# Two-layer graph network on 12,500 nodes: six tiles a round gathered ahead instead of three, and source counts compared against a row in PSUM

## The reference, cut to what matters

```python
def _L0_gnn_ref(feat, W1, W2, b, src, dst):
    out_deg = jnp.maximum(jax.ops.segment_sum(ones, src, num_segments=n), 1.0)
    in_cnt = jax.ops.segment_sum(ones, dst, num_segments=n)
    t1 = feat @ W1
    msg = t1[src] + feat[src] * feat[dst] @ W2
    scale = jnp.sqrt(out_deg[src]) * jnp.sqrt(out_deg[dst])
    agg = jax.ops.segment_sum(msg / scale[:, None], dst, num_segments=n)
    embed = jnp.where(in_cnt[:, None] > 0, t1 + agg, jnp.zeros_like(t1)) + b
    embed = jax.nn.leaky_relu(embed, negative_slope=0.01)
    return embed / jnp.maximum(jnp.linalg.norm(embed, axis=1, keepdims=True), 1e-12)

def _L1_gnn_ref(x, W, b, edge_index):
    src, tgt = (edge_index[0], edge_index[1])
    xt = jnp.einsum('ni,oi->no', x, W) + b
    out = jax.ops.segment_sum(xt[src], tgt, num_segments=num_nodes)
    deg = jax.ops.segment_sum(jnp.ones_like(tgt, dtype=x.dtype), tgt, num_segments=num_nodes)
    return out / (deg + 1.0)[:, None]

x = _layernorm(x + _L0_gnn_ref(x, L0_gnn_W1, L0_gnn_W2, L0_gnn_b, src, dst), axis=-1)
x = _layernorm(x + _L1_gnn_ref(x, L1_gnn_W, L1_gnn_b, edge_index), axis=-1)
```

## Time and profile before

| | us |
|---|---|
| median of three runs | 4066.2 |
| lowest and highest run | 4062.96, 4067.36 |
| span of the profiled execution, first to last instruction | 4061.9 |
| GpSimd busy | 3038.5 (75%) |
| TensorE busy, matmuls | 3098.3 (76%) |
| VectorE busy | 1691.2 (42%) |
| mean granted TensorE clock, share of full speed | 0.758 |

### The profile page before, as it was taken

How to read it: one execution, slowest core, us unless ns; L and a number is a source line. 1 busy time by engine, 2 the same in 40 slices (tenths; PEclk the granted TensorE clock), 3 DMA queues, 4 the chain that set the end, 5 groups by cost and what they waited for, 6 DMA issues and landing times.

```text
span 4061.9 us, 41375 instructions
## 1 busy us (share of the span) xinstructions
PE 3098.3 (76%) x9904; PEld 1794.2 (44%) x9904; DVE 1691.2 (42%) x3546; ACT 518.9 (13%) x1597; POOL 3038.5 (75%) x3147
## 2 busy tenths in 40 slices
PE   6527777777777777777768887887888787888887
PEld 5414554455455554545434443333444343344433
DVE  9934444444444554444432333333332333333323
ACT  8911111111111111111100000000000000000000
POOL 7867777777777777777757777777777777777776
PEclk8758888888888888888866677767676767666666
DMA  7584444444444444444424434344444444444443
GB/s 253 157 280 133 138 131 132 138 138 135 134 133 138 138 133 135 133 138 137 124 86 115 120 115 120 115 120 115 120 117 118 117 118 117 117 119 116 120 115 106
DMA packets 281951, 536.08 MB, mean 132 GB/s; under 512 B 60499, under 2 KB 181892, under 8 KB 281924
## 3 DMA queue, kind: packets, MB, share of 16 engines
q0 software_dynamic: 150048, 409.93, 35.3%
q1 hardware_dynamic: 119204, 112.98, 8.7%
q10 hardware_dynamic: 12672, 12.85, 0.9%
HBM read 478.55 MB, written 56.97 MB: 132 GB/s over the span
## 4 chain that ended last, share of the span: by engine, by line
POOL 69%; issue 24%; PE 2%; SPq 1%; DMA 1%; DVE 1%; POOLq 1%; DVEq 1%; ACT 0%; ACTq 0%
POOL ring L474 65%; POOL ring L482 4%; SPq L321 1%; PE banks L1116 1%; PE banks L1090 1%; DVEq L678 1%; DMA ring<-scaled_x,idx 0%; POOLq L503 0%; POOLq L471 0%; DMA ring<-in_x,src_col 0%; POOLq L472 0%; DMA ring<-in_dst 0%; DVE stats L903 0%; SPq L287 0%; DVE out_t L899 0%
## 5 line engine op out<-in xcount | busy, mean ns | idle before, releaser
L1116 PE MATMUL banks<-ring,hot_space 128*128 128x257 f32 x6252 | 2628.9, 542 | 852.9 <-DMA ring<-scaled_x,idx 389.4
L1116 PEld LDWEIGHTS banks<-ring,hot_space 128*128 128x128 f32 x6252 | 1328.2, 249 | 2077.5 <-DMA ring<-x,idx 1053.7
L474 POOL DMA_INDIRECT ring<-x,idx x1563 | 1487.2, 951 | 504.6 <-issue 475.9
L474 POOL DMA_INDIRECT ring<-scaled_x,idx x1422 | 1350.7, 950 | 442.5 <-issue 440.1
L836 DVE SCALAR_TENSOR_TENSOR big<-banks,here_mask,big 128x257 f32 x784 | 343.7, 480 | 1833.5 <-PE banks L1116 1833.4
L796 DVE TENSOR_TENSOR hot_space<-banks,dst_rel 128x1024 f32<-128x1024 f32 x395 | 483.6, 1225 | 210.1 <-issue 207.1
L582 ACT COPY idx<-src_col 128x8 int32 (+1 forms) x392 | 77.3, 197 | 2350.1 <-PE banks L1116 2350.1
L482 POOL DMA_INDIRECT ring<-in_x,src_col x141 | 196.0, 1390 | 57.4 <-issue 42.4
L1090 PE MATMUL banks<-w_s,a_t 128*128 128x256 f32 x784 | 187.0, 394 | 0.0
L1090 PEld LDWEIGHTS banks<-w_s,a_t 128*128 128x128 f32 x784 | 156.6, 200 | 23.8 <-ACT a_t L604 0.4
L546 ACT ACTIVATE dst_rel<-columns,halves 128x128 bf16<-128x128 f32 x576 | 161.3, 375 | 3.2 <-DVE halves L715 3.2
(11 more groups left out here) (115 smaller groups left out, 958.7 us busy)
## 6 DMA issues: line engine op xcount, KB each, us to landing
ring<-x,idx POOLq DMA_INDIRECT x1563, 2.8
ring<-scaled_x,idx POOLq DMA_INDIRECT x1422, 2.8
kept_rows<-ring SPq DMA_DIRECT2D x141, 128.0 KB, 3.3
ring<-kept_rows SPq DMA_DIRECT2D x47, 384.0 KB, 3.8
x<-out_t SPq DMA_DIRECT2D x98, 128.0 KB, 2.4
x_t<-x SPq DMA_DIRECT2D x98, 128.0 KB, 2.2
x_t<-in_x SPq DMA_DIRECT2D x97, 128.0 KB, 2.2
result<-out_t SPq DMA_DIRECT2D x97, 128.0 KB, 1.9
```

The costliest lines, as they stand in the source:

```text
L474: g.indirect_dma_start(ring[:, u, 0:D], None, table[layer], bass.IndirectOffsetOnAxis(ap=idx[:, u:u + 1], axis=0)).then_inc(rows_in[u], 16)
L1116: last = nc.tensor.matmul(group_sum(k % SUMS), dst_hot[:, k % HOTS, u - k * GT, :], ring[:, u, 0:DW], start=u == tiles[0], stop=u == tiles ...
```

## The change

1. `KEPT` goes from 3 to 6. 282 tiles are gathered early, and rounds 1 to 47 of layer 0 gather 26 tiles where they gathered 29. The load of kept rows, their scaling, and the look-up of `r_kept` become twice as wide.
2. Kept tiles are gathered into blocks of three that lie side by side in the flat `ring` (11 blocks, `UNITS`), and a block goes out with one store of 384 KB, 94 stores in all.
3. The comparisons of the source counts take a row of numbers that stands in PSUM (`lane_row`) in place of the table `count_to` in SBUF, and lay their results out one tile behind the other. There are 70 such batches where there were 80, and 112 batches of signs where there were 72. TensorE's loop over them is written out.
4. The edges are staged in the last columns of x's own buffer, so that `ring` is free from the start; the first six kept tiles read their source numbers from `first_src`, loaded by a DMA of its own ahead of the edges.
5. x is loaded, scaled and stored in 14 chunks of 7 blocks where there were 8 of up to 14.
6. The memset of the ones in `ring` waits for the last kept store.

```diff
@@ -46,12 +46,10 @@
 HB = 16
-PAIR = 2
 SB = 4
-STEP_BATCHES = 72
+STEP_BATCHES = 112
...
-SPANS = 8
@@ -64,15 +62,18 @@
 FINAL = -(-EDGES // P) - (ROUNDS - 1) * U
-X_CHUNKS = [(w, min(w + 14, NW)) for w in range(-8, NW, 14)]
-X_CHUNKS[0] = (0, X_CHUNKS[0][1])
...
-KEPT = 3
+X_CHUNKS = [(w, w + 7) for w in range(0, NW, 7)]
...
+KEPT = 6
...
-SLOTS = 16
-BASES_AT = 82
+UNIT = 3
+KEPT_UNITS = KEPT_TILES // UNIT
+UNITS = U * PITCH // (UNIT * D)
+X_EVERY = 4
+BASES_AT = 78
+NAT_AT = NW * D - 4 * BLOCKS * P
@@ -98,8 +99,11 @@
         ring_flat = ring[:, :, :].rearrange("p u f -> p (u f)")
-        nat = [ring_flat[:, n * BLOCKS * P:(n + 1) * BLOCKS * P] for n in range(2)]
-        nat_i = [ring_flat[:, (2 + n) * BLOCKS * P:(3 + n) * BLOCKS * P].bitcast(I32) for n in range(2)]
+        early = [ring_flat[:, n * UNIT * D:(n + 1) * UNIT * D] for n in range(UNITS)]
+        staging = big[:, NAT_AT:NW * D]
+        nat = [staging[:, n * BLOCKS * P:(n + 1) * BLOCKS * P] for n in range(2)]
+        nat_i = [staging[:, (2 + n) * BLOCKS * P:(3 + n) * BLOCKS * P].bitcast(I32) for n in range(2)]
+        first_src = sb("first_src", [P, KEPT], I32)
@@ -107,16 +111,14 @@
         place_hot = dst_col[:, 0:KE]
-        place_low = dst_col[:, KE:2 * KE].bitcast(I32)
-        place_src = dst_col[:, 2 * KE:3 * KE].bitcast(I32)
-        count_to = sb("count_to", [P, P, PAIR], BF16)
+        place_src = dst_col[:, KE:2 * KE].bitcast(I32)
...
-            "p (h a n c) -> p h a n c", h=2, a=HB // PAIR, c=PAIR)
+            "p (h t n) -> p h t n", h=2, t=HB)
...
-        lo_hot = [hot[:, n, :, 0:P, :] for n in range(2)]
-        hi_hot = [hot[:, n, :, P:P + HI, :] for n in range(2)]
+        lo_hot = [hot[:, n, :, 0:P] for n in range(2)]
+        hi_hot = [hot[:, n, :, P:P + HI] for n in range(2)]
@@ -156,8 +158,9 @@
         out_t = [sb(f"out_t{n}", [P, D]) for n in range(2)]
-        sums_t = sb("sums_t", [P, 2, DW])
-        block_hot = sums_t[:, :, :].rearrange("p s f -> p (s f)")[:, 0:KEPT * NW].rearrange("p (t n) -> p t n", t=KEPT)
+        sums_space = sb("sums_space", [P, KEPT * NW])
+        sums_t = sums_space[:, 0:2 * DW].rearrange("p (s f) -> p s f", s=2)
+        block_hot = sums_space[:, :].rearrange("p (b t n) -> p b t n", b=2, t=UNIT)
@@ -176,7 +179,7 @@
         project = [banks[:, 6, s * D:(s + 1) * D] for s in range(2)]
-        found = banks[:, 2, 0:KEPT * NW].rearrange("p (t n) -> p t n", t=KEPT)
+        found = banks[:, 2:4, 0:UNIT * NW].rearrange("p b (t n) -> p b t n", t=UNIT)
@@ -278,6 +282,8 @@
                 sp.sem_inc(stored[s], 16)
+            sp.dma_start(first_src[:, :], src[U * P:U * P + KE].rearrange("(t p) -> p t", p=P),
+                         allow_slow_non_contiguous=True).then_inc(first_in, 16)
@@ -288,10 +294,10 @@
                              edges[FULL_TILES * P:EDGES].rearrange("(p e) -> p e", p=1)).then_inc(edges_loaded[n], 16)
-            sp.wait_ge(x_padded, 1)
...
+                if end * D > NAT_AT:
+                    sp.wait_ge(x_padded, 1)
@@ -316,16 +322,16 @@
             def store_kept(n):
-                slot = n % SLOTS
-                sp.wait_ge(early_in[slot], 16 * (n // SLOTS + 1))
-                sp.dma_start(kept[n // KEPT, :, n % KEPT * D:(n % KEPT + 1) * D],
-                             ring[:, slot, 0:D]).then_inc(kept_out[slot], 16)
-
-            for n in range(KEPT_TILES):
+                place, half = n % UNITS, n % (KEPT // UNIT)
+                sp.wait_ge(early_in[place], 16 * UNIT * (n // UNITS + 1))
+                sp.dma_start(kept[n * UNIT // KEPT, :, half * UNIT * D:(half + 1) * UNIT * D],
+                             early[place]).then_inc(kept_out[place], 16)
+
+            for n in range(KEPT_UNITS):
                 store_kept(n)
-                if n % 4 == 1 and n // 4 < len(X_CHUNKS):
-                    load_x_chunk(*X_CHUNKS[n // 4])
-                if n == 4 * len(X_CHUNKS):
+                if n % X_EVERY == 0 and n // X_EVERY < len(X_CHUNKS):
+                    load_x_chunk(*X_CHUNKS[n // X_EVERY])
+                if n == X_EVERY * len(X_CHUNKS):
@@ -476,19 +480,23 @@
             def gather_kept(n):
-                slot, tile = n % SLOTS, (n // KEPT + 1) * U + n % KEPT
-                if n >= SLOTS:
-                    g.wait_ge(kept_out[slot], 16 * (n // SLOTS))
-                g.indirect_dma_start(ring[:, slot, 0:D], None, x,
-                                     bass.IndirectOffsetOnAxis(ap=src_col[:, tile:tile + 1], axis=0)
-                                     ).then_inc(early_in[slot], 16)
-
+                place, t = n // UNIT % UNITS, n % UNIT
+                if t == 0 and n >= UNITS * UNIT:
+                    g.wait_ge(kept_out[place], 16 * (n // (UNITS * UNIT)))
+                tile = (n // KEPT + 1) * U + n % KEPT
+                sources = first_src[:, n:n + 1] if n < KEPT else src_col[:, tile:tile + 1]
+                g.indirect_dma_start(early[place][:, t * D:(t + 1) * D], None, x,
+                                     bass.IndirectOffsetOnAxis(ap=sources, axis=0)).then_inc(early_in[place], 16)
+
+            g.wait_ge(first_in, 16)
+            for n in range(KEPT):
+                gather_kept(n)
+            g.wait_ge(edges_in_cols, 1)
+            for n in range(KEPT, KEPT_TILES):
+                gather_kept(n)
+            for place in range(UNITS):
+                g.wait_ge(kept_out[place], 16 * len(range(place, KEPT_UNITS, UNITS)))
             g.wait_ge(idx_ready, 4)
-            g.wait_ge(step_digits_made, 1)
-            for n in range(KEPT_TILES):
-                gather_kept(n)
-            for slot in range(SLOTS):
-                g.wait_ge(kept_out[slot], 16 * len(range(slot, KEPT_TILES, SLOTS)))
@@ -551,6 +559,8 @@
                     step_batch(3 * b + third, third)
+            for n in range(STEP_BATCHES // 3 * 3, STEP_BATCHES):
+                step_batch(n, n % 3)
@@ -681,10 +691,9 @@
                 for digit, hots, size in ((src_lo, lo_hot, P), (src_hi, hi_hot, HI)):
-                    vals = digit[:, bass.ds(batch * HB, HB)].rearrange("p (a c) -> p a c", c=PAIR)
-                    shape = [P, HB // PAIR, size, PAIR]
-                    last = nc.vector.tensor_tensor(hots[half], vals.unsqueeze(2).to_broadcast(shape),
-                                                   count_to[:, 0:size, :].unsqueeze(1).to_broadcast(shape), ALU.is_equal)
+                    vals = digit[:, bass.ds(batch * HB, HB)]
+                    last = nc.vector.tensor_tensor(hots[half], lane_row[:, 0:size].unsqueeze(1).to_broadcast([P, HB, size]),
+                                                   vals.unsqueeze(2).to_broadcast([P, HB, size]), ALU.is_equal)
@@ -715,7 +723,11 @@
             last.then_inc(step_digits_made, 1)
-            v.wait_ge(consts_made, 17)
+            v.wait_ge(consts_made, 16)
+            v.wait_ge(edges_in_cols, 2)
+            nc.vector.tensor_copy(lane_row, columns[:, :])
+            nc.vector.memset(x_all[:, NW - 1, :], 0.0).then_inc(x_padded, 1)
+            ordered()
@@ -800,13 +810,14 @@
                 v.wait_ge(places_in, 16 * i)
-                nc.vector.tensor_scalar(place_low[:, :], place_src[:, :], P - 1, None, ALU.bitwise_and)
+                nc.vector.tensor_scalar(place_src[:, :], place_src[:, :], P - 1, None, ALU.bitwise_and)
                 ordered()
-                nc.vector.tensor_scalar(place_hot[:, :], place_low[:, :], lane[:, 0:1], None,
+                nc.vector.tensor_scalar(place_hot[:, :], place_src[:, :], lane[:, 0:1], None,
                                         ALU.is_equal).then_inc(places_made, 1)
-                blocks = src_hi[:, bass.ds(i * U, KEPT)].unsqueeze(2).to_broadcast([P, KEPT, NW])
-                nc.vector.tensor_tensor(block_hot, lane_row[:, 0:NW].unsqueeze(1).to_broadcast([P, KEPT, NW]),
-                                        blocks, ALU.is_equal)
+                shape = [P, 2, UNIT, NW]
+                blocks = src_hi[:, bass.ds(i * U, KEPT)].rearrange("p (b t) -> p b t", b=2)
+                nc.vector.tensor_tensor(block_hot, lane_row[:, 0:NW].unsqueeze(1).unsqueeze(1).to_broadcast(shape),
+                                        blocks.unsqueeze(3).to_broadcast(shape), ALU.is_equal)
@@ -814,7 +825,7 @@
                 ordered()
-                nc.vector.tensor_reduce(r_kept[:, bass.ds(i * KEPT, KEPT)], found, AX.X,
+                nc.vector.tensor_reduce(r_kept[:, bass.ds(i * KEPT, KEPT)].rearrange("p (b t) -> p b t", b=2), found, AX.X,
@@ -824,6 +835,9 @@
                 group_hot(g * GT, g)
+            for place in range(UNITS):
+                v.wait_ge(kept_out[place], 16 * len(range(place, KEPT_UNITS, UNITS)))
+            nc.vector.memset(ring[:, :, D:DW], 1.0).then_inc(ring_ones, 1)
@@ -1039,18 +1052,10 @@
             pe.wait_ge(edges_in_cols, 2)
-            def span(n, first, last_one):
-                per_span, steps_per_span = SRC_BATCHES // SPANS, STEP_BATCHES // SPANS
```

(25 more changed lines are left out.)

12 lines of the change are left out of this document (4 added, 8 removed).

## The result

| | before | after | forecast |
|---|---|---|---|
| median of four runs, us | 4066.4 (4063.0 to 4067.4) | 3995.0 (3994.0 to 3996.8) | 3997 (3985 to 4040) |
| span of the profiled execution, us | 4061.9 | 3995.1 | 3993 |
| first gather from `scaled_x`, us | 268.9 | 374.2 | 376 |
| first gather of layer 1, us | 2081.3 | 2014.7 | |

The ratio is 0.9828, with a 95% interval of 0.9816 to 0.9839: the changed kernel is faster by 1.7%. By stages, from the three time stamps and the spans: the early phase is 105.3 us longer (forecast 107), layer 0 went from 1812.4 to 1640.5 us, 171.9 less (forecast 176), layer 1 from 1980.6 to 1980.4. Together that is 66.8 us of span, where 69 were forecast.

What follows compares the result with a forecast made beforehand. The prediction took GpSimd's gathers as the bound, with VectorE holding them back beside the counts. +107 us in the early phase and -176 in layer 0 make -69, span 3993; plus 4.3 for the median, 3997 us (3985 to 4040).

Steps and rivals of the forecast that it cites:

- Part 1: Layer 0: 141 gathers leave at 1.25 us each, -176 us if GpSimd stays the bound; a round lasts 32.6 us.
- part 5: Layer 0 rounds: doubled kept load, scaling and look-up add nothing; hold-up of gathers taken as zero, up to 66 us possible.
- Part 2: Source counts on VectorE: comparisons lose double rate, a pair costs 3.92 us, 70 pairs 274.5 us; counts end at 295 us.
- Part 3: Early phase, scaling and storing x: first x store at 305 us, first scaled gather at 376, where it stood at 268.9.
- Part 4: Early phase: kept gathers run at 1.25 us each, last ends at 362.5; x stores end last, by some 4 us.
- The sum: Whole kernel: +107 and -176 make -69 us, span 3993; median 4.3 us above the span, so 3997 us.
- The rival on TensorE: Layer 0: TensorE becomes the bound, records sum to 32.6 us a round; loss 0.05, round of 33 to 34 us 0.08.
- The rival of the held gathers: Early phase: kept gathers stay at 2.02 us beside the counts, total 4097 us; chance 0.05.

Runs made afterwards that it cites:

- e1: Changed kernel, source counts compared with the f32 row `columns` in SBUF instead of its PSUM copy: 4094.7 us.
- e6: Changed kernel with ten more batches of source counts on VectorE and TensorE (80 batches, some tiles counted twice): 4019.0 us.
- e7: Changed kernel with ten batches of source counts left out (60 batches, 160 tiles not counted): 3990.8 us, median of four.
- e4: Changed kernel, rounds 1 to 47 of layer 0 leave out three more gathers (23 a round), TensorE still multiplying 32 tiles: 3821.9 us.
- e5: Changed kernel, rounds 1 to 47 of layer 0 leave out six more gathers (20 a round): 3808.8 us.
- e2: Kernel before, with only the source counts' comparison moved to the row in PSUM: 4211.8 us against 4062.3.

## Why the prediction was right, point by point

- **Part 1, the rounds.** Forecast -176, measured -171.9 in layer 0. The mechanism held: no gather waited for `idx`. The term that was mis-sized is the zero of part 5. A gather takes 954 ns in the mean where it took 950, and the gathers over 0.98 us number 65 in the trace of 8 x 210 us, with 9.8 us more than the undisturbed value between them, where the kernel before had 42 with 5.7. That is the 4 us. The trace shows where most of it comes from: 23 gathers of layer 0, 2.8 us over the undisturbed value together, end 0.12 us behind the end of the two look-up operations at L813 and L815, which are 768 wide now; none did so in the kernel before, where they were 384 wide (352 and 460 ns). One of the 23 ends at 1241.04, 0.12 us behind 1240.92:

```profile
1239.97 1.07 POOL L478 DMA_INDIRECT ring<-scaled_x,idx  x1 [0.30 <-issue]
1240.30 0.62 DVE L815 TENSOR_SCALAR dst_col<-dst_col,lane 128x768 f32<-128x768 int32 x1
```

  No run took these operations out.
- **Part 2, the counts.** A pair of comparisons cost (292.6 - 19.8) / 70 = 3.90 us, forecast 3.92; the slope from two rows of other operations on PSUM was enough. The counts ended at 292.6, not 295.2. Of these 2.6 us, 1.7 are 70 pairs that are 0.02 us shorter each, and 0.9 is the start: I had charged 0.8 us for the 768 pieces of `first_src`, and the edges were in no later than before (the first cast at 6.86 us, before at 7.10).
- **Part 3, scaling and storing.** First store at 304.4 (forecast 305), and it is that close by luck: the counts ended 2.6 us early, and from their end to the first store it took 11.8 us where 10.0 were worked out. The scaling got shorter as forecast; what was missed is 1.7 us in which VectorE waits for TensorE's last products, a wait that the kernel before does not have. From the first store to the first scaled gather it took 69.8 us (forecast 70.8), by the bytes and the rate that were worked out.
- **Part 4, the kept gathers.** 946 ns beside the counts, the last ending at 361.5 (forecast 362.5). e1 shows the reason, which had only been argued from the earlier trace rows. That the two paths lie close together was right too (e6, e7). Which of them ends last was wrong: the x stores were to end last by some 4 us, and the last kept store landed 0.9 us behind them. The 9.6 us taken over from the kernel before for what follows the last kept gather were 12.8, since its landing and its store now share the DMA engines with the x stores (the rows landed 6.1 us after the gather's end, and the store took 4.3 us to land, where e7 has 2.3). The two paths draw on the same bytes, so this did not change the sum.
- **Part 5, twice the kept work.** The kept load grew to 768 KB and lands in 5.5 us, the wait of TensorE for the scaled rows from 2.2 to 3.5 us a round; neither reached the end.
- **The sum.** The span was to be 3993 and was 3995.1; the median was to lie 4.3 us above it and lies 0.1 below. In every run of the result the time is 1.7 us above that run's own span; the rest of the 4.3 was that the profiled execution of the kernel before was faster than its median run. The early phase came out 2 us better and layer 0 some 4 us worse than forecast. So a miss of 2 us in the median is in part luck.
- **The rival on TensorE** named a round of 32.6 us as the sum of the records at their old pace. The pace did change, as the text against it said: 0.30 us a record, at a granted clock of 0.87. e4 and e5 put the floor at 28.8, where 28.2 was worked out.
- **The rival of the held gathers** (4097 us) is e1, and it came out at 4094.7. Its price was right; its condition was not met.

## What to carry to other kernels

When GpSimd's gathers are the bound, look at what VectorE runs beside them: beside comparisons with both tensor inputs in SBUF one gather came through every 1.95 to 2.02 us here, and moving one input to PSUM brought that to 1.25 us even though VectorE then took nearly twice as long. Price such an edit by the gathers that can use the freed time, not by the engine it slows: here it cost 117 us alone and brought 57 beside more work for GpSimd. And when a phase grows longer, look in every queue for a wait that stands in the middle of a stream because it used to be over by then (e2).

## What the runs showed of the hardware that was not expected

A gather that meets a two-input comparison is held at its beginning, for as long as the comparison runs, and finishes 0.90 us after the next instruction starts; one that meets a cast at double rate ends 0.11 us behind the cast's end, as at 328 to 330 us in the changed kernel:

```profile
328.06 0.98 DVE L793 TENSOR_SCALAR hot_space<-hot_space 128x1568 int32<-128x1568 int32 x1
328.41 1.79 POOL L488 DMA_INDIRECT ring<-in_x,src_col  x1 [0.30 <-issue]
329.11 0.98 DVE L795 CAST dst_rel<-hot_space 128x1568 f32<-128x1568 int32 x1
```

(329.11 + 0.98 = 330.09, and 328.41 + 1.79 = 330.20.) So in these two cases the price of a neighbour on VectorE depends on how its length stands to the 1.25 us of a gather: comparisons of 1.2 and 1.0 us let one gather pass in 2.02 us, comparisons of 2.3 and 1.8 us one in 1.95 us, nearly the same although they are nearly twice as long.
